# Two graph layers over one 4096 x 4096 adj: node order and tile shape of the adj loads

## What is computed

```python
h  = relu(layernorm(x))
h  = proj(mobius_add(proj(mobius_matvec(W, h)), bias))   # row-wise, hyperbolic
xt = logmap0(h)                                          # 4096 x 128 "tangents"
s  = adj @ xt                                            # the first large product
x1 = x + proj(expmap0(relu(logmap0(proj(expmap0(s))))))  # row-wise again
h2 = relu(layernorm(x1))
left, right = (context @ Wc.T) @ w_left + b_left, (context @ Wc.T) @ w_right + b_right
logits = leaky_relu(left[:, None] + right[None, :], 0.2)
logits = where(adj <= 0, -inf, logits)
out = x1 + relu(softmax(logits, axis=-1) @ h2)
```

## Time and profile before

| what | value |
|---|---|
| timed runs, us | 686.53, 689.55, 690.34; median 689.55 |
| profiled execution, its span | 684.8 us; its own time beside the span isn't recorded |
| phase 1, to the last adj product | about 0 to 398 us of the span |
| busy share: PE, DVE, ACT, POOL | 76%, 80%, 62%, 33% |
| moved by DMA | 84.51 MB, mean 123 GB/s |
| HBM read, written | 79.96 MB, 4.21 MB |

### The profile page before, as it was taken

One profiled execution on the slowest core, in us unless ns is written; L12 is line 12 of the kernel. 1 busy time (PEld: TensorE's weight loads), 2 busy tenths in 40 slices (PEclk: granted clock), 3 DMA queues, 4 the chain that ended last, 5 costly groups with the idle time before them and its releaser, 6 DMA issues. The chain is left out here.

```text
span 684.8 us, 9734 instructions
## 1 busy us (share of the span) xinstructions
PE 517.0 (76%) x2695; PEld 308.5 (45%) x2695; DVE 549.3 (80%) x1057; ACT 422.9 (62%) x553; POOL 226.9 (33%) x217
## 2 busy tenths in 40 slices
PE   1702689887785687778788855577999989898995
PEld 1601124232231232323223234466878778787875
DVE  4888998766954456566575689999999999999995
ACT  3943466453453344546444488839898888888891
POOL 5808960664721414406000155831011010202020
PEclk9955899999999799999999989999999999999999
DMA  9993479999999999999999900010101011111010
GB/s 182 219 223 68 105 149 215 213 220 215 213 226 122 176 223 213 225 223 227 220 221 220 214 26 25 8 32 16 33 16 33 16 31 33 26 33 31 0 31 15
DMA packets 164235, 84.51 MB, mean 123 GB/s; under 512 B 7248, under 2 KB 163152, under 8 KB 164208
## 3 DMA queue, kind: packets, MB, share of 16 engines
q1 hardware_dynamic: 163520, 83.91, 67.9%
q0 software_dynamic: 256, 0.15, 0.1%
q10 hardware_dynamic: 432, 0.13, 0.1%
HBM read 79.96 MB, written 4.21 MB: 123 GB/s over the span
## 5 line engine op out<-in xcount | busy, mean ns | idle before, releaser
L619 PE MATMUL ps<-room 128*128 128x512 f32 x512 | 261.6, 643 | 98.4 <-DVE room L884 60.2
L884 DVE STREAM_TRANSPOSE room<-room 128x512 f32<-128x512 f32 x256 | 169.2, 691 | 104.3 <-DMA room<-in_adj_dram 96.0
L758 ACT ACTIVATE mask<-room 128x1024 f32 (+1 forms) x128 | 135.0, 1055 | 168.5 <-DVE room L884 167.1
L619 PEld LDWEIGHTS ps<-room 128*128 128x128 f32 x512 | 91.7, 199 | 262.8 <-DVE room L884 180.4
L645 PE MATMUL ps<-room 128*128 128x258 f16 x1152 | 136.6, 279 | 31.7 <-DVE room L1126 31.7
L645 PEld LDWEIGHTS ps<-room 128*128 128x128 bf16 x1152 | 112.4, 99 | 54.8 <-DVE room L1126 37.9
L645 PE MATMUL ps<-room,mask 128*128 128x258 f16 x896 | 101.2, 273 | 9.9 <-DVE h_room L1140 6.7
L645 PEld LDWEIGHTS ps<-room,mask 128*128 128x128 bf16 x896 | 86.2, 97 | 23.7 <-DVE h_room L1140 8.1
L797 ACT ACTIVATE room<-mask 128x2048 bf16 (+1 forms) x36 | 68.5, 1903 | 12.4 <-PE ps L645 12.3
L554 POOL TENSOR_TENSOR h_room<-h_room 128x512 f32<-128x512 f32 x7 | 9.9, 1409 | 145.4 <-DVE post L1151 145.4
L797 ACT ACTIVATE mask<-mask 128x2048 bf16 (+1 forms) x28 | 53.3, 1903 | 4.7 <-PE ps L645 4.7
(11 more groups left out here) (164 smaller groups left out, 557.3 us busy)
## 6 DMA issues: line engine op xcount, KB each, us to landing
room<-in_adj_dram SPq DMA_DIRECT2D x256, 256.0 KB, 7.1
mask<-in_L_gnn_context_dram SPq DMA_DIRECT2D x16, 256.0 KB, 10.7
mask<-in_x_dram SPq DMA_DIRECT2D x16, 128.0 KB, 5.7
xk<-in_x_dram SPq DMA_DIRECT2D x32, 64.0 KB, 5.1
out_dram<-xk SPq DMA_DIRECT2D x32, 64.0 KB, 4.6
h_room<-out_dram SPq DMA_DIRECT2D x32, 64.0 KB, 2.6
out_dram<-h_room SPq DMA_DIRECT2D x28, 64.0 KB, 1.8
room<-neg_left SPq DMA_DIRECT2D x4, 256.0 KB, 3.7
```

What stands on the lines that cost most here:

```text
L619: pe.matmul(acc[parity], xt[:, k, :], turned[:, k % TSLOTS, :], start=(k == 0), stop=(k == NK - 1)).then_inc(block_multiplied, 1)
L758: nc.scalar.activation(mc[:, half * HB:(half + 1) * HB, :], turned[:, slots:slots + HB, :], ACT.Sign).then_inc(half_signed, 1)
L884: v.transpose(turned[:, k % TSLOTS, :].rearrange("p (l b i) -> p b l i", l=L, b=NQ), loaded[:, g % XSLOTS, :, l * Q:(l + 1) * Q].rearrange ...
```

## The change

The node numbering becomes (b l s q): the partition group b is the slowest part, then the block in a chunk, then the chunk s. So a row chunk is 16 runs of 32 rows, 256 rows apart. On the column side each group of 32 partitions owns 1024 adjacent columns, and a tile takes XB x Q = 256 of them. A tile is 512 rows x 1024 columns (2 MB), 16 rows by 256 columns a partition, so a contiguous run is 1 KB. There are NT = 4 tiles of XB = 8 blocks in a chunk, and XSLOTS = 2 slots, in the same 32 KB of each partition. Column block k of the stream is now node block `node(k)` = k % 8 * 4 + k // 8, so xt, the scales and the mask are addressed by `node(k)`. SP stores x1 behind tile 0 and loads x behind tile 1.

```diff
-XSLOTS = 4
+XSLOTS = 2
+XB = 8
...
+    NT = NK // XB
...
-        loaded = view(room, o, [XSLOTS, L * NQ, L * Q], F32)
-        o += XSLOTS * CH * L * 4
+        loaded = view(room, o, [XSLOTS, L * NQ, XB * Q], F32)
+        o += XSLOTS * CH * XB * 4
...
-            return t.rearrange("(s b l q) d -> s b q l d", b=NQ, l=L, q=Q)
+            return t.rearrange("(b l s q) d -> s b q l d", b=NQ, l=L, q=Q)
...
-        x_l, cx_l = (t.rearrange("(s b l q) d -> l b q s d", b=NQ, l=L, q=Q) for t in (x, context))
-        adj_n = adj.rearrange("(s r p) (g b j) -> s g b p r j", r=CH // Q, p=Q, b=NQ, j=L * Q)
+        x_l, cx_l = (t.rearrange("(b l s q) d -> l b q s d", b=NQ, l=L, q=Q) for t in (x, context))
+        adj_n = adj.rearrange("(r s p) (b g j) -> s g b p r j", s=NC, p=Q, b=NQ, j=XB * Q)
+
+        def node(n):
+
+            return n % XB * L + n // XB
...
-                for g in range(NC):
+                for g in range(NT):
                     if not (isinstance(c, int) and c == 0 and g < XSLOTS):
 
-                        sp.wait_ge(block_turned, c * NK + L * (g - XSLOTS + 1))
+                        sp.wait_ge(block_turned, c * NK + XB * (g - XSLOTS + 1))
...
-                    if g == 1 and not (isinstance(c, int) and c < 2):
+                    if g == 0 and not (isinstance(c, int) and c < 2):
                         store_x1(c - 2)
-                    if g == 3 and not (isinstance(c, int) and c < 1):
+                    if g == 1 and not (isinstance(c, int) and c < 1):
                         load_x(c - 1)
...
-            sp.wait_ge(block_turned, NC * NK - (XSLOTS - 1) * L)
+            sp.wait_ge(block_turned, NC * NK - (XSLOTS - 1) * XB)
...
-                    pe.matmul(acc[parity], xt[:, k, :], turned[:, k % TSLOTS, :],
+                    pe.matmul(acc[parity], xt[:, node(k), :], turned[:, k % TSLOTS, :],
...
-                    nc.scalar.activation(mc[:, half * HB:(half + 1) * HB, :], turned[:, slots:slots + HB, :],
+                    first = node(half * HB)
+                    nc.scalar.activation(mc[:, first:first + L + 1:L, :], turned[:, slots:slots + HB, :],
                                          ACT.Sign).then_inc(half_signed, 1)
...
-                g, l = k // L, k % L
+                g, l = k // XB, k % XB
                 if l == 0:
-                    dve.wait_ge(adj_in[g % XSLOTS], c * (16 * NQ * NC // XSLOTS) + 16 * NQ * (g // XSLOTS + 1))
+                    dve.wait_ge(adj_in[g % XSLOTS], c * (16 * NQ * NT // XSLOTS) + 16 * NQ * (g // XSLOTS + 1))
...
-                        tangent(k)
+                        tangent(k, node(k))
```

More of the change, by code:

```diff
@@ L96, in bass_two_graph_layers @@
         XT_BYTES = NK * D * 4
-        phase_1_bytes = XT_BYTES + XSLOTS * CH * L * 4 + TSLOTS * CH * 4
+        phase_1_bytes = XT_BYTES + XSLOTS * CH * XB * 4 + TSLOTS * CH * 4
         phase_2_bytes = 2 * NK * GW * 2 + 3 * 2 * L * CH * 2
@@ L139, in bass_two_graph_layers @@
         nl_at = XT_BYTES
-        assert nl_at == 4 * half_slot and (NC - XSLOTS) % XSLOTS == 0
+        assert nl_at == 4 * half_slot and NT % XSLOTS == 0
         nl_even = view(room, nl_at, [CH], F32)
@@ L324, in load @@
                 rows = pick(adj_n, c)
-                for g in range(NC):
+                for g in range(NT):
                     if not (isinstance(c, int) and c == 0 and g < XSLOTS):
-                        sp.wait_ge(block_turned, c * NK + L * (g - XSLOTS + 1))
+                        sp.wait_ge(block_turned, c * NK + XB * (g - XSLOTS + 1))
                     for b in range(NQ):
-                        sp.dma_start(loaded[b * Q:(b + 1) * Q, g % XSLOTS], rows[g, b]).then_inc(
-                            adj_in[g % XSLOTS], 16)
+                        sp.dma_start(loaded[b * Q:(b + 1) * Q, g % XSLOTS], rows[g, b]).then_inc(adj_in[g % XSLOTS], 16)
                     if isinstance(c, int) and c == 0 and g == XSLOTS - 1:
                         load_nodes(cx, cx_l, cx_in)
-                    if g == 1 and not (isinstance(c, int) and c < 2):
+                    if g == 0 and not (isinstance(c, int) and c < 2):
                         store_x1(c - 2)
-                    if g == 3 and not (isinstance(c, int) and c < 1):
+                    if g == 1 and not (isinstance(c, int) and c < 1):
                         load_x(c - 1)
@@ L708, in bias_part @@
                     act.wait_ge(xt_ready, k - XT_AHEAD + 1)
-                nc.scalar.activation(fb[:, k % XT_AHEAD, :], hb, ACT.Copy, scale=sv[:, 14, k:k + 1]).then_inc(
+                at = node(k)
+                nc.scalar.activation(fb[:, k % XT_AHEAD, :], hb, ACT.Copy, scale=sv[:, 14, at:at + 1]).then_inc(
                     fb_ready, 1)
@@ L969, in _, with tangent @@
             dve.wait_ge(tangent_scales, 1)
-            def tangent(k):
-                dve.wait_ge(fb_ready, k + 1)
+            def tangent(n, k):
+                dve.wait_ge(fb_ready, n + 1)
                 v.scalar_tensor_tensor(out=xt[:, k, :], in0=mx[:, k, 0:D], scalar=T1[:, k:k + 1],
-                                       in1=fb[:, k % XT_AHEAD, :], op0=ALU.mult, op1=ALU.add).then_inc(xt_ready, 1)
+                                       in1=fb[:, n % XT_AHEAD, :], op0=ALU.mult, op1=ALU.add).then_inc(xt_ready, 1)
             POST = 6
```

## The result

The changed kernel takes 823.07 us (819.33 to 836.11, four runs) against 689.71: ratio 1.192, 95% interval 1.186 to 1.198 (the run of 836.11 was in a slower state of the core and is left out of the ratio). I had forecast 697.0, with a range of 683 to 707. The sign was right and the size was far off: 133 us instead of 7.5.

What follows compares the result with a forecast made beforehand. The first half, to about 398 us, was taken as bound by the adj loads, the attention half by DVE. -4.9 + 4.7 + 3.7 + 4 = +7.5 us on 689.55 gave 697.0 us, range 683 to 707.

Steps and rivals of the forecast that it cites:

- Part 1, the rate: Adj loads in the first half: packets of 1 KB instead of 512 B raise 219 to 223 GB/s, -4.9 us.
- Part 3, the renumbering: x, context, out, xt, mask, transposes and neg_left under the new numbering: taken as 0, with up to -6 us kept.
- Part 2, the ring: Adj loads in two 2 MB slots instead of four of 1 MB: costs of 4.7, 3.7 and 4 us.
- The tail: After the last adj tile lands, eight blocks are turned and multiplied instead of four: +3.7 us.
- the head start: Before the tangent scales are known, 16 blocks are preloaded instead of 20; one tile moves behind the idle time: +4.7 us.
- The gaps: DMA idles between tiles where GpSimd's products slow DVE, in chunks 1 and 2: four places, +4 us, bounds 0 and 12.
- a limit that goes with partitions and not packets: Adj loads: the limit goes with bytes, not packets; a cited port rule gives partitions 0 to 31 about 218 GB/s.
- The rivals: Loads really faster, 684.8 us (0.17); costs cancel, 688.6 (0.15); two slots starve the queue, 712 (0.10); packets not 1 KB, 702 (0.03).
- The two slots starve the queue: Rival on the adj loads: no gain in rate and a 0.4 us gap at each tile, +23 us, 712 us; chance 0.10.
- low rate of 213: Lower bound in GB/s for the new adj loads, from the page's low slices: +7.7 us instead of -4.9.

Runs made afterwards that it cites:

- experiments 8 and 9: 8: the kernel before with partition groups issued 0, 2, 1, 3, 678.24 us; 9: the kernel before with groups 2 and 3 issued from ScalarE's queue, 644.79 us.
- experiment 1: The changed kernel with a row chunk again 512 adjacent rows, so row pieces lie 512 KB apart instead of 4 MB: 706.14 us.

## Why the prediction was right or wrong

- **Part 1, the rate, failed.** The step took 223 GB/s from context, "same packets, same partitions, full queue". It compared packet size and destination, and never the source. Context's eight rows of a partition lay 512 KB apart, as adj's did; the new adj pieces lie 4 MB apart. The streams measured 131 to 176 GB/s. Where 275 us at 223 had stood for -4.9, the far rows cost +117 (823 against 706). The gain of 4.9 didn't come with near rows either: 706 against 701, a difference within the noise.
- **Part 3, the renumbering, failed for the same reason.** It went through x, xt, the mask, the transposes and neg_left, and left out the one access pattern with 67 MB. "x, context and out still go in rows of 512 B or 1 KB" was right and beside the point. The diff shows it: `(s r p)` becomes `(r s p)`.
  The Trainium skill had the rule (DMA: Bandwidth & Descriptors, Latency and other measured facts, HBM row pitch at large powers of two): copies between HBM tensors run at 207 GB/s with a row pitch of 512 KiB, 164 with 2 MiB and half with 4 MiB. This case, with loads into SBUF, agrees in order, 198 to 218, 165 to 183 and 131 to 159 GB/s in stretches behind 102 us, and adds that it isn't the distance, as 3.5 MB runs at 190 to 217. An estimate by the figures of that page, 219 x 103 / 207, would have had adj at 109 GB/s: slower than measured, but on the right side.
- **Part 2, the ring, was right as a sum.** 12.4 us forecast, 11.5 measured alone (8 to 19). The tail is seen (7.86 us of products at the end), and so is the head start: 4 GB/s from 53 to 57 us where the kernel before has 196. The gaps, put at 4 us, come to about 7 by an estimate from the profiles: 206 GB/s in place of 211 over the 288 us from 102 to 390.
- **That 1 KB packets bring little was right for this queue order:** 706 against 701. The reason, a limit that goes with partitions and not packets, is supported: reordering the groups moved it, and so did splitting them over queues (experiments 8 and 9), while packet size on one queue did not. But it holds for DMAs that follow each other; I hadn't seen that it is a limit which the kernel could leave.
- **The rivals.** None was the cause. "The two slots starve the queue" looked most like the trace, with SP waiting 141.7 us, and is refuted as the main cause: experiment 1 has 213.1 us of such waits and takes 706 us. A rival of the form "the loads get slower, as their source is another" was missing altogether. The range's low rate of 213 came from slices of the same access pattern, so it couldn't hold this.

The kernels in a row: 690 before, 701 with the coarse ring (+11.5), 706 with 1 KB packets and the new columns as well (+4.9, within the noise), 823 with the far rows (+117). These are differences along one path, so that they add up to 133 us proves nothing more. Far rows and a coarse ring might make each other dearer: far rows at 1 KB with four slots weren't tried.

## What to carry to other kernels

When a change gives a load another shape, compare all of its access pattern, source strides first: how many different places within a large power of two (4 MB in the count used here) do the pieces in flight fall on? A stream at its limit isn't always at the chip's limit: ask which partitions it fills at one time, and try filling both halves (partitions 0 to 63 and 64 to 127) from two queues before touching packet sizes. A queue that waits for slots tells little by itself; the rate into empty slots tells more.

## What the runs showed of the hardware that I hadn't expected

- Loads for 32 partitions, one behind the other on one queue, give 217 to 224 GB/s; ordered 0, 2, 1, 3, 224 to 227; groups 0, 1 and groups 2, 3 on two queues, 255 to 276.
- Row pieces on one place within 4 MB give 126 GB/s at 512 B and 176 (159 in another kernel) at 1 KB, before any slot is waited for; on eight places 217 and 213.
- A second queue doesn't raise the rate on far rows: 131 and 116 GB/s with two queues, 158 and 134 with one, in the same stretches.
- The mean time of a 1 KB packet hardly rises with far rows (91 ns for 88); one in twenty takes over 235 ns for 101, and the engines have fewer packets in hand (share 0.98 for 1.14 in the first stretch).
